# A gated expert layer on one core: from eight down products per chunk pair to seven, with weight forms kept in DRAM

## The reference

```python
def _L0_cond_ref(hidden_states, gating_probs, shared_gate_prob, Wg, Wu, Wd, Sg, Su, Sd):
    E, B, S, D, F = (8, 2, 256, 256, 1024)
    h = hidden_states
    g = jnp.einsum('bsd,edf->ebsf', h, Wg)
    u = jnp.einsum('bsd,edf->ebsf', h, Wu)
    expert_outs = jnp.einsum('ebsf,efd->ebsd', jax.nn.silu(g) * u, Wd)
    expert_output = jnp.einsum('be,ebsd->bsd', gating_probs, expert_outs)
    shared = jnp.einsum('bsf,fd->bsd', jax.nn.silu(h @ Sg) * (h @ Su), Sd)
    sg = shared_gate_prob[:, :, None]
    return (1.0 - sg) * expert_output + sg * shared
```

## Time and profile before

| | |
|---|---|
| median of 3 runs | 2179.14 us (2177.81 to 2179.55) |
| profiled execution | 2178.35 us, its span 2176.5 us |
| matmuls | 9504 |
| busy share of PE, DVE, ACT, POOL | 99%, 68%, 70%, 64% |
| transfers | 122.22 MB, mean 56 GB/s |

### The profile page before, as it was taken

One profiled execution on the slowest core, in us unless ns is written; L12 is line 12 of the kernel. 1 busy time (PEld: TensorE's weight loads), 2 busy tenths in 40 slices (PEclk: granted clock), 3 DMA queues, 4 the chain that ended last, 5 costly groups with the idle time before them and its releaser, 6 DMA issues.

```text
span 2176.5 us, 34574 instructions
## 1 busy us (share of the span) xinstructions
PE 2159.4 (99%) x9504; PEld 1785.0 (82%) x9504; DVE 1490.3 (68%) x2623; ACT 1532.3 (70%) x2623; POOL 1386.7 (64%) x2046
## 2 busy tenths in 40 slices
PE   7999999999999999999999999999999999999999
PEld 5888888888888888888888888888888888888887
DVE  6666666666766666666676666666667666666666
ACT  7767776776777677767777776777677677767775
POOL 7766666666866666666686666666666666666663
PEclk9999999999999999999999999999999999999999
DMA  4111111111211111111121111111112111111110
GB/s 151 59 51 56 52 51 51 58 51 51 72 57 51 51 57 51 51 51 58 51 71 54 55 51 51 58 51 51 51 58 70 52 54 54 51 51 58 51 51 27
DMA packets 44683, 122.22 MB, mean 56 GB/s; under 512 B 5088, under 2 KB 5344, under 8 KB 44640
## 3 DMA queue, kind: packets, MB, share of 16 engines
q1 hardware_dynamic: 44640, 121.73, 18.0%
HBM read 117.51 MB, written 4.19 MB: 56 GB/s over the span
## 4 chain that ended last, share of the span: by engine, by line
PE 99%; DMA 0%; SPq 0%; POOL 0%; DVE 0%; ACT 0%; issue 0%; DVEq 0%; ACTq 0%
PE chain_ps L274 12%; PE down_ps L274 12%; PE down_ps L275 12%; PE down_ps L276 12%; PE chain_ps L275 12%; PE chain_ps L276 12%; PE p_ps L275 6%; PE p_ps L274 6%; PE p_ps L276 6%; PE p_up_ps L275 3%; PE p_up_ps L274 3%; PE p_up_ps L276 3%; DMA acc<-xT 0%; POOL w_lo L205 0%; SPq L145 0%
## 5 line engine op out<-in xcount | busy, mean ns | idle before, releaser
L205 POOL TENSOR_TENSOR w_lo<-w_raw,w_hi 128x384 fp32r<-128x384 f32 x861 | 850.8, 1019 | 731.5 <-ACT w_hi L374 731.5
L190 POOL TENSOR_TENSOR w_raw<-w_raw 128x128 f32<-128x128 f32 x1148 | 506.9, 464 | 32.6 <-DMA w_raw<-w 10.1
L274 PE MATMUL chain_ps<-x_hi,w_hi 128*128 128x512 f32 x1152 | 449.4, 390 | 11.7 <-DVE w_lo L590 5.8
L275 PE MATMUL chain_ps<-x_lo,w_hi 128*128 128x512 f32 x1152 | 448.6, 389 | 0.0
L276 PE MATMUL chain_ps<-x_hi,w_lo 128*128 128x512 f32 x1152 | 448.6, 389 | 0.0
L274 PE MATMUL down_ps<-h_hi,w_hi 128*128 128x512 f32 x1152 | 448.2, 389 | 0.2 <-DVE h_lo L508 0.2
L275 PE MATMUL down_ps<-h_lo,w_hi 128*128 128x512 f32 x1152 | 448.1, 389 | 0.0
L276 PE MATMUL down_ps<-h_hi,w_lo 128*128 128x512 f32 x1152 | 448.1, 389 | 0.0
L374 ACT CAST w_hi<-w_raw 128x768 fp32r<-128x768 f32 (+1 forms) x574 | 387.3, 675 | 85.1 <-PE down_ps L276 78.8
L395 ACT CAST h_hi<-p_up_ps 128x512 fp32r<-128x512 f32 x288 | 169.0, 587 | 307.8 <-DVE p_up_ps L493 307.8
L516 DVE TENSOR_TENSOR gate<-tap_p,p_up_ps 128x512 f32<-128x512 f32 x288 | 198.0, 687 | 251.0 <-PE p_up_ps L276 251.0
(11 more groups left out here) (47 smaller groups left out, 2852.6 us busy)
## 6 DMA issues: line engine op xcount, KB each, us to landing
w_raw<-w SPq DMA_DIRECT2D x287, 384.0 KB, 3.0
outT<-acc SPq DMA_DIRECT2D x7, 512.0 KB, 4.4
acc<-xT SPq DMA_DIRECT2D x6, 512.0 KB, 9.4
...
```

Of the source, the lines that this page charges most:

```text
L190: nc.gpsimd.tensor_tensor(raw[:, cols(dst, dst)], raw[:, cols(a, a)], raw[:, cols(b, b)], op).then_inc(w_sums, 1)
L205: ins = nc.gpsimd.tensor_tensor(w_lo[:, s, c], w_raw[:, s, c], w_hi[:, s, c].bitcast(F32), ALU.subtract)
L274: nc.tensor.matmul(bank, w_hi[:, s, c], hi, start=start, stop=False, **on)
L275: nc.tensor.matmul(bank, w_hi[:, s, c], lo, start=False, stop=False, **on)
```

## The change

Token pair 0 keeps its unit, but everything that it makes of the weights is also stored to DRAM: for every unit the 7 forms of gate and up in both parts (`kept_gate`, 896 KB), and for every pair of chunks 7 forms of the down weights (`kept_down`, 896 KB), four of which are new sums of the blocks of two chunks (`down_sums`, `down_hi`, `down_lo`). In token pairs 1 to 3 no weight is loaded raw and none is summed or split: SP fetches the kept forms (`fetch`).

There the loop body is a pair of chunks (`two_groups`). The h of two chunks and two tiles form a 2x2 block matrix, and the down step of the pair is made of 7 products q1 to q7 instead of 8. For these, h needs 7 forms too: four sums (T1 to T4, `h_t1` to `h_t4`, on POOL), and high and low parts in `h_forms` (ACT; DVE for B11, B22, B21, POOL for T1 to T4). q2 to q5 add up in one bank each over the whole token pair. q1, q6 and q7 share the fifth bank `side_ps`, in which each goes on from the one before, and DVE adds the bank to `acc` or `u3_sum` after each (`tap`). At the end of a token pair DVE adds the four banks and `u3_sum` to `acc` (`finish_q`, and two more adds).

Gate and up do with three banks. ACT copies p1 from one bank of `chain_ps` to the other (`seed`), p2 goes on from the copy, and the Silu reads it there. DVE writes the sum u4 back into `p53_ps`, p3 goes on from it, and the Silu of tile 1 works in place. The memory of token pair 0's buffers is used again under other names.

The core of the diff: what SP stores and fetches, POOL's work on h, PE's products and their order, then ACT and DVE in a chunk pair. `q(number, *before, ...)` is the down step of the chunk pair before.

```diff
+            def keep(e, k):
+                n = group(0, e, k)
+                s, j = k % SLOTS, k // 2
+                if k % 2 == 1:
+                    sp.wait_ge(d_lo_done, e * PAIRS + j + 1)
+                elif isinstance(n, int) and n == 0:
+                    sp.wait_ge(w0_lo_done, 4)
+                else:
+                    sp.wait_ge(w_lo_done, n)
+                for part, forms in enumerate((w_hi, w_lo)):
+                    sp.dma_start(kept_of(kept_gate, e, k, part, 0, GATE_FORMS - 1), w_cols(forms, s, A11, S4).bitcast(F32)).then_inc(
+                        kept_stored[s], 16
+                    )
+                    first, last = (DA11, DA11) if k % 2 == 0 else (DA12, DA22)
+                    sp.dma_start(
+                        kept_of(kept_down, e, j, part, first, last), w_cols(forms, s, D0, D0 + last - first).bitcast(F32)
+                    ).then_inc(kept_stored[s], 16)
+                if k % 2 == 1:
+                    for part, sums in enumerate((d_hi, d_lo)):
+                        sp.dma_start(
+                            kept_of(kept_down, e, j, part, DS1, DS4), sums[:, j % 2].bitcast(F32)
+                        ).then_inc(sums_stored[j % 2], 16)
+
...
+            def fetch(g, e, k):
+                sp.wait_ge(p4_done, group(g, e, k) - 3)
+                fetch_gate(e, k)
+                if k % 2 == 1:
+                    sp.wait_ge(q_done[3], pair(g, e, k // 2) - 1)
+                    fetch_down(e, k // 2)
...
+            def h_pair(g, e, j):
+                n, pc = group(g, e, 2 * j), pair(g, e, j)
...
+                if started:
+                    pool.wait_ge(h1_done, n)
+                    pool.wait_ge(h_summed[T1], pc)
...
+                    subtract(h_t2[:], h_b1[:], h_t1[:]).then_inc(h_summed[T2], 1)
+                    pool.wait_ge(h0_done, n)
+                    pool.wait_ge(h_summed[T2], pc)
+                    subtract(h_t4[:], h_b0[:], h_t2[:]).then_inc(h_summed[T4], 1)
+                    subtract(h_t3[:], h_b1[:], h_a1[:]).then_inc(h_summed[T3], 1)
+                    form_lo_of(T2, 6, pc)
+                    form_lo_of(T4, 4, pc)
...
+                    form_lo_of(T3, 7, pc)
...
+                pool.wait_ge(h1_done, n + 1)
+                pool.wait_ge(h0_done, n + 1)
...
+                subtract(h_t1[:], h_a1[:], h_a0[:]).then_inc(h_summed[T1], 1)
...
+                form_lo_of(T1, 5, pc + 1)
...
+            Q_OF = {1: (DA11, B11), 2: (DA12, B21), 3: (DS4, B22), 4: (DA22, T4), 5: (DS1, T1), 6: (DS2, T2), 7: (DS3, T3)}
...
+            def q(number, g, e, j, pc):
+
+                w_form, h_form = Q_OF[number]
+                pe.wait_ge(form_lo[h_form], pc + 1)
...
+                    pe.wait_ge(down_loaded[j % 2], 16 * uses)
+                    after(pe, tapped[7], pc)
+                elif number == 6:
+                    pe.wait_ge(tapped[1], pc + 1)
+                elif number == 7:
+                    pe.wait_ge(tapped[6], pc + 1)
+                weights = two(down_slot[j % 2], w_form)
+                moving = h_forms[:, H_AT[h_form]], h_forms[:, H_AT[h_form] + 1]
+                if number in SUM_BANK:
+                    start = is_first(e, j)
+                    if start and g == 1:
+                        pe.wait_ge(added[0 if number in (2, 4) else 1], 1)
+                    elif start:
+                        pe.wait_ge(finished[number], g - 1)
+                    last = isinstance(e, int) and e == EXPERTS - 1 and j == PAIRS - 1
+                    ins = product(SUM_BANK[number], weights, moving, start=start, stop=last)
+                else:
+                    ins = product(side_ps[:], weights, moving, start=number == 1, stop=True, goes_on=number != 1)
+                ins.then_inc(q_done[number], 1)
...
+                def p6(n, k):
+                    pe.wait_ge(p1_seeded, n - PER + 1)
+                    product(
+                        chain_ps[:, k % 2, :], fetched(k % SLOTS, S2), x_of(g, T2, first and k == 0), start=False, stop=True, goes_on=True
+                    ).then_inc(p6_done, 1)
+
...
+                ka, kb = 2 * j, 2 * j + 1
+                p4(g - 1 if first else g, (ka - 1) % CHUNKS, na - 1)
+                p1(na, ka)
+                p5(na, ka)
+                down_step(1, 0, CHUNKS - 2, 0)
+                p6(na, ka)
+                down_step(5, 0, CHUNKS - 2, 1)
+                p2(ka)
+                p7(na, ka)
+                p3(ka)
+                p1(nb, kb)
+                p4(g, ka, na, first=first)
+                down_step(6, 1, CHUNKS - 1, 0)
+                p5(nb, kb)
+                down_step(4, 1, CHUNKS - 1, 1)
+                p6(nb, kb)
+                p2(kb)
+                down_step(7, 0, CHUNKS - 1, 0)
+                p7(nb, kb)
+                p3(kb)
+                down_step(2, 0, CHUNKS - 1, 1)
+                down_step(3, None, None, None)
...
+            def silu1(n):
+                act.wait_ge(p3_done, n + 1)
+                nc.scalar.activation(p53_ps[:], p53_ps[:], ACT.Silu).then_inc(silu_done[1], 1)
...
+                def seed(n, k):
+                    act.wait_ge(p1_done, n + 1)
+                    if opening and k == 0:
+                        act.wait_ge(h_lo_done[0], n)
+                    else:
+                        act.wait_ge(h0_done, n)
+                    nc.scalar.copy(chain_ps[:, 1 - k % 2, :], chain_ps[:, k % 2, :]).then_inc(p1_seeded, 1)
...
+                def silu0(n, k):
+                    act.wait_ge(p2_done, n + 1)
+                    act.wait_ge(h0_done, n)
+                    nc.scalar.activation(silu[:, 0], chain_ps[:, 1 - k % 2, :], ACT.Silu).then_inc(silu_done[0], 1)
...
+                else:
+                    silu1(na - 1)
...
+                    form_hi_of(B22, 3, h1_done, na, pc - 1)
+                seed(na, 2 * j)
+                tap5(na)
+                if not opening:
+                    form_hi_of(T2, 6, h_summed[T2], pc, pc - 1)
+                    form_hi_of(T4, 4, h_summed[T4], pc, pc - 1)
+                silu0(na, 2 * j)
+                if not opening:
+                    form_hi_of(T3, 7, h_summed[T3], pc, pc - 1)
+                next_x(g, e, 2 * j)
+                silu1(na)
+                seed(nb, 2 * j + 1)
+                tap5(nb)
+                if not opening:
+                    form_hi_of(B21, 2, h0_done, na, pc - 1)
+                silu0(nb, 2 * j + 1)
+                next_x(g, e, 2 * j + 1)
+                form_hi_of(B11, 1, h0_done, nb, pc)
+                form_hi_of(T1, 5, h_summed[T1], pc + 1, pc)
...
+            def u4(n, k):
+                dve.wait_ge(p6_done, n + 1)
+                dve.wait_ge(p5_tapped, n + 1)
+                plus(p53_ps[:], tap_p5[:], chain_ps[:, k % 2, :]).then_inc(u4_done, 1)
+
+            def up1(n, k):
+                dve.wait_ge(p7_done, n + 1)
+                plus(silu[:, 1], tap_p5[:], chain_ps[:, k % 2, :]).then_inc(up1_done, 1)
...
+            def form_lo_of(form, count, full=None):
+                dve.wait_ge(form_hi[form], count)
+                full = h_full[form][:] if full is None else full
+                minus(h_forms[:, H_AT[form] + 1], full, h_forms[:, H_AT[form]].bitcast(F32)).then_inc(form_lo[form], 1)
+
+            def tap(number, g, pc, first):
+
+                dve.wait_ge(q_done[number], pc + 1)
+                if number == 7 and first:
+                    ins = nc.vector.tensor_copy(u3_sum[:], side_ps[:])
+                else:
+                    into = {1: acc[:, 2 * g, 0, :], 6: acc[:, 2 * g + 1, 0, :], 7: u3_sum[:]}[number]
+                    ins = plus(into, side_ps[:], into)
+                ins.then_inc(tapped[number], 1)
...
+                else:
+                    form_lo_of(B11, pc)
+                    up1(na - 1, ka - 1)
...
+                    h1(gp, ep, na - 1, h_b1[:])
+                    h0(gp, ep, ka - 1, na - 1, h_b0[:])
+                    form_lo_of(B22, pc)
+                u4(na, ka)
+                if not opening:
+                    tap(1, gp, pc - 1, False)
+                up1(na, ka)
...
+                else:
+                    dve.wait_ge(h_summed[T3], pc)
+                h1(g, e, na, h_a1[:])
+                h0(g, e, ka, na, h_a0[:])
+                if not opening:
+                    tap(6, gp, pc - 1, False)
+                if first and g > 1:
+                    finish_q(5, gp, [acc[:, 2 * gp + 1, c, :] for c in range(DC)])
+                u4(nb, kb)
+                if not opening:
+                    form_lo_of(B21, pc)
+                    tap(7, gp, pc - 1, is_first(ep, jp))
+                else:
+                    add(1)
+                if first and g == 1:
+                    pass
+                elif first:
+                    finish_q(4, gp, [acc[:, 2 * gp, 1, :]])
+                    dve.wait_ge(tapped[7], gp * PER_PAIRS)
+                    dve.wait_ge(finished[5], gp)
+                    for t in (1, 0):
```

(44 more changed lines are left out.)

819 lines of the change are left out of this document (571 added, 248 removed).

## The result

The changed kernel takes 2183.91 us (median of 19 runs, 2182.41 to 2186.22) against 2178.97 us of the kernel before: ratio 1.0023, 95% interval 1.0016 to 1.0030. It is slower by 0.2%, where I had forecast 2122 us.

The account below looks back on a forecast made before the run. PE, busy 99% of the span, was taken as the bound, so matmuls must go. 2178.35 - 73.4 + 16.0 = 2121.0, with 0.8 for the median 2122 us; range 2108 to 2155, about 8 in 10.

Parts of the forecast that it names:

- PE at full pitch: Steady matmul stream on PE: 0.2267 us per matmul, so 14.28 us for the 63 matmuls of a chunk pair.
- What is removed: Down step in token pairs 1 to 3: 7 products instead of 8 per chunk pair, 324 matmuls, 73.4 us less.
- Does PE never wait?: Chunk pairs of token pairs 1 to 3: hand-overs fit with least slack 0.10 us, so 14.28 us per pair.
- rival B: Seed path before p6 of the second chunk exceeds its 0.10 us slack; at most 45 us, 2167, middle 2143; 19%.
- rival C: DVE and POOL block each other on SBUF at B11's low part; 0.83 us per chunk pair, 90 us, 2211; 7%.
- x forms: Where x forms are made, a Silu is pushed by 0.2 us in a few pairs: 0.6 us lost.
- rival D: Stores of token pair 0 don't keep up; at 200 GB/s 98 us more, 2219; 4%.
- What is lost: Waits at the three changeovers, the end and x forms: 4.0 + 6.0 + 5.4 + 0.6 = 16.0 us.
- into token pair 1: Changeover: the seed waits for h0's last low part, 1.2 us, and up1 comes late behind DVE, 2.8 us.
- into token pairs 2 and 3: Changeovers: seven more DVE adds delay PE 2.3 us, up to 1.3 more from POOL; 3.0 each, 6.0.
- end: Last products and adds wait on each other: 10.3 us against some 4.9 before, 5.4 more.
- rival A: PE keeps full pitch in chunk pairs, with losses as forecast; 2112 to 2133 us; 60%.

Follow-up runs that it names:

- e2: Changed kernel with the tile warm widened from 1 to 16 elements (64 bytes), so w_raw and all tiles behind start at a multiple of 128 bytes; 2135.99 us.

## Why the prediction was wrong, point by point

**The step that failed** is the one that looks like no step: "PE at full pitch", 9180 matmuls at 0.2267 us. I took 0.2267 from rows 3 as the price of a matmul. It is the price with operands that start alike, as those of the kernel before happened to do. The changed kernel has 0.2324, and 47.9 us of its time come from the place of its tiles (changed against e2). No rival of mine held it; my list of what would prove me wrong named only a recurring wait, and none is there.

**What is removed**: right. 9180 matmuls; e2 has the 73.4 us.

**Does PE never wait?** Right. With like starts e2 takes 14.30 us from 1399.17 to 1413.47, between equal matmuls:

```profile
1399.17 0.39 PE L542 MATMUL chain_ps<-x_hi,gate_forms 128*128 128x512 f32 x1
...
1413.47 0.39 PE L542 MATMUL chain_ps<-x_hi,gate_forms 128*128 128x512 f32 x1
```

I had 14.28. The extra 0.02 lies in front of p6 of the second chunk in nearly every pair: rival B's place, at a twentieth of its upper bound. The instructions that no row had shown were not dear. Changed kernel, groups by shape (busy us, mean ns, idle before):

```profile
L852 ACT ACTIVATE p_ps<-p_ps 128x512 f32<-128x512 f32 x216 | 125.7, 582 | 76.8 <-PE p_ps L544 76.8
L865 ACT COPY chain_ps<-chain_ps 128x512 f32<-128x512 f32 x216 | 123.1, 570 | 291.0 <-DVE h_a L956 201.3 <-DVE h_b L956 88.8 <-DVE h_lo L965 0.8
```

**The lock** (rival C): right in the steady state, too small elsewhere. The low parts of h average 0.74 and 0.72 us in the changed kernel against 0.68 undisturbed. But where POOL also makes x forms, they meet. DVE and POOL of e2:

```profile
596.64 1.81 DVE L965 TENSOR_TENSOR h_forms<-h_b,h_forms 128x512 fp32r<-128x512 f32 x1
...
598.98 1.80 DVE L965 TENSOR_TENSOR h_forms<-h_a,h_forms 128x512 fp32r<-128x512 f32 x1
```

and

```profile
596.60 1.30 POOL L384 TENSOR_TENSOR x_sum<-acc,x_sum 128x512 f32<-128x512 f32 x1
598.94 1.30 POOL L384 TENSOR_TENSOR h_forms<-h_t,h_forms 128x512 fp32r<-128x512 f32 x1 [1.03 <-ACT h_forms L848]
```

Each DVE instruction starts 0.04 us behind a POOL one of 1.30 us and takes 1.1 us longer than the undisturbed 0.68. The Trainium skill, "SBUF — State Buffer", section "SBUF: two separate sides", says just that of such a pair, and the rows agree. The two together made up1 1.3 us late, and PE waited for it; that happens three times, 4.3 us. I had looked for the lock only between the h forms, and had 0.6 us for x forms. The stretches with them lose 6.8 us in e2.

**Token pair 0** (rival D): right. 0.2267 us a matmul at 235 GB/s.

**What is lost**, counted in e2 as spacing beyond 0.2267 against the kernel before:

| term | said | e2 |
|---|---|---|
| start | 0 | 1.6 |
| into token pair 1 | 4.0 | 5.1 |
| into token pairs 2 and 3 | 6.0 | 10.3 |
| x forms (590 to 680 and 1110 to 1200 us) | 0.6 | 6.8 |
| end | 5.4 | 4.9 |
| small steps in the other chunk pairs | 0 | 4.1 |
| sum | 16.0 | 32.8 |

2176.5 - 73.4 + 32.8 = 2135.9, and e2's span is 2135.8. In each of the changeovers into token pairs 2 and 3 3.4 are the wait and 1.7 the granted clock at 1.2 instead of 2.4 GHz behind it: from 1095.95 to 1097.23 three steps take 1.28 us, 0.43 each. I had priced the idle time and not the matmuls behind it.

So without the placement the forecast of 2122 would have been 14 us too low. The 2136.0 of e2 lies inside my range of 2108 to 2155, but outside the 2112 to 2133 of rival A, whose mechanism it shows: only the room kept for rival B, which came at a twentieth of its size, holds it. That is luck. One chance was also added up wrong: slower had 0.10, less than the 0.07 and 0.04 of C and D alone.
